# Second scan of a two-layer kernel: the output rows are turned by VectorE in 32x32 blocks instead of by TensorE

## What is computed

```python
x = x + _L0_conv_ref(_gn(x), ...)      # per head: a 128x128 softmax matrix mixes the 128 positions; plus a bias
x = x + _L1_conv_ref(_gn(x), W)        # a scan over h:
# rows = moveaxis(x, 1, 0); row0 = rows[0]
# def step(carry, row):
#     new = row + relu(conv1d_same(carry, W))     # W is (9, 64, 64), along the 128 positions
#     return new, new
```

## Time and profile before

| | us |
|---|---|
| median of 3 runs | 833.74 |
| lowest, highest | 831.69, 834.27 |
| the profiled execution, its own time | 832.51 |
| its span | 830.5 |
| TensorE busy | 740.7 (89%) |
| VectorE busy | 593.0 (71%) |
| ScalarE busy | 479.2 (58%) |
| GpSimd busy | 433.3 (52%) |
| TensorE's granted clock, mean | 0.978 of full speed |

### The profile page before, as it was taken

How to read it: one execution, slowest core, us unless ns; L and a number is a source line. 1 busy time by engine, 2 the same in 40 slices (tenths; PEclk the granted TensorE clock), 3 DMA queues, 4 the chain that set the end, 5 groups by cost and what they waited for, 6 DMA issues and landing times.

```text
span 830.5 us, 17386 instructions
## 1 busy us (share of the span) xinstructions
PE 740.7 (89%) x5546; PEld 705.0 (85%) x5546; DVE 593.0 (71%) x1265; ACT 479.2 (58%) x918; POOL 433.3 (52%) x416
## 2 busy tenths in 40 slices
PE   1577667758999999999999999998999999999997
PEld 1456555648999899999999998988999999999997
DVE  6699999983767878786878787655555555555553
ACT  2156555564666676666666666656555555555552
POOL 1666777762656566656656565643333333333332
PEclk9999999997999999999999999999999999999999
DMA  9845444231334443444434321212222222222222
GB/s 184 157 103 122 108 102 108 45 77 37 85 83 102 91 102 89 91 91 102 101 89 101 87 66 42 52 39 52 65 65 64 63 63 63 63 63 67 66 65 68
DMA packets 203149, 68.11 MB, mean 82 GB/s; under 512 B 137556, under 2 KB 203092, under 8 KB 203092
## 3 DMA queue, kind: packets, MB, share of 16 engines
q1 hardware_dynamic: 203092, 67.43, 37.2%
HBM read 33.85 MB, written 33.55 MB: 81 GB/s over the span
## 4 chain that ended last, share of the span: by engine, by line
PE 73%; DVE 15%; issue 4%; POOL 4%; ACT 2%; DVEq 0%; ACTq 0%; POOLq 0%
PE ps_conv L976 37%; PE ps_conv L980 18%; PE ps_mix L892 7%; PE ps_out L968 7%; DVE st L668 4%; PE ps_in L905 4%; DVE st L550 3%; POOL xs L352 3%; DVE dev L613 2%; PE ps_small L882 1%; DVE x_sb L661 1%; ACT x_paired L438 1%; ACT rows L460 1%; DVE st L562 1%; DVE dev L618 1%
## 5 line engine op out<-in xcount | busy, mean ns | idle before, releaser
L379 POOL TENSOR_TENSOR total<-x_paired,carry 128x256 f32<-128x256 f32 x256 | 188.7, 737 | 305.1 <-DVE carry L758 301.7
L766 DVE TENSOR_TENSOR carry_l<-carry,carry_h 128x256 fp32r<-128x256 f32 x252 | 174.6, 693 | 90.9 <-ACT carry_h L480 90.9
L480 ACT ACTIVATE carry_h<-carry 128x256 fp32r<-128x256 f32 x252 | 105.7, 419 | 228.3 <-DVE carry L758 228.1
L976 PE MATMUL ps_conv<-carry_h,wh 128*128 128x256 f32 x1280 | 219.5, 303 | 5.3 <-ACT carry_h L480 5.3
L438 ACT ACTIVATE x_paired<-ps_in,shift 64x512 f32<-64x512 f32 (+1 forms) x256 | 174.8, 683 | 75.9 <-PE ps_in L905 72.6
L352 POOL TENSOR_TENSOR xs<-x_sb,rstd 128x512 f32<-128x512 f32 x104 | 195.1, 1898 | 38.6 <-DVE rstd L643 38.6
L976 PE MATMUL ps_conv<-carry_h,wl 128*128 128x256 f32 x1280 | 198.3, 285 | 0.0
L980 PE MATMUL ps_conv<-carry_l,wh 128*128 128x256 f32 x1280 | 197.0, 285 | 0.0
L976 PEld LDWEIGHTS ps_conv<-carry_h,wh 128*128 128x128 f32 x1280 | 176.9, 192 | 7.1 <-ACT carry_h L480 5.9
L758 DVE SCALAR_TENSOR_TENSOR carry<-ps_conv,rows 128x256 f32<-128x256 f32 x256 | 107.7, 421 | 105.0 <-PE ps_conv L980 98.9
L976 PEld LDWEIGHTS ps_conv<-carry_h,wl 128*128 128x128 f32 x1280 | 174.5, 191 | 0.0
(11 more groups left out here) (92 smaller groups left out, 401.4 us busy)
## 6 DMA issues: line engine op xcount, KB each, us to landing
out_dram<-staged SPq DMA_DIRECT2D x256, 128.0 KB, 2.4
x_sb<-in_x_dram SPq DMA_DIRECT2D x52, 512.0 KB, 4.1
rows<-in_x_dram SPq DMA_DIRECT2D x12, 512.0 KB, 4.0
x_paired<-in_L_conv_W_dram SPq DMA_DIRECT2D x2, 80.0 KB, 2.7
x_paired<-in_L_conv_W_dram SPq DMA_DIRECT2D x2, 64.0 KB, 2.5
x_paired<-v_attention_centers_dram SPq DMA_DIRECT2D x1, 0.0 KB
x_paired<-v_attention_spreads_dram SPq DMA_DIRECT2D x1, 0.0 KB
bias_col<-v_token_proj_n_bias_dram SPq DMA_DIRECT2D x1, 0.5 KB, 5.3
```

Of the source, the lines that this page charges most:

```text
L379: nc.gpsimd.tensor_tensor(total[s][:, :].rearrange("p (w j) -> p w j", w=WS), x1_rows(wave, it, i, 1, s * WS, WS)[:, 0, :, :], carry[s][:, ...
L766: nc.vector.tensor_tensor(carry_l[s][:, :, EDGE:EDGE + J], carry[s][:, :].rearrange("p (w j) -> p w j", w=WS), carry_h[s][:, :, EDGE:EDGE ...
L976: nc.tensor.matmul(ps_conv[:, s * BANK:s * BANK + SW], w[:, d, :], carry_h[s][:, :, d:d + J], start=(w is wh and d == 0), stop=False)
```

## The change

In the second scan (wave 1) the four TensorE transposes and ScalarE's copy go. VectorE transposes `total[s]` in 32x32 blocks straight into `staged` (`flip_out`), between the carry of a half and its low part. After it a partition of `staged` holds a position, and a run of 32 elements holds 32 channels. Eight DMAs store a row, each from 32 partitions, 8 batches, 128 contiguous bytes at a time (256 runs of 128 bytes). SyncE issues five of them, ScalarE three, behind its second norm of the step. GpSimd's next sum waits for the flip of its half. A flip waits for the stores of the row two before (`flip_stored`). VectorE's first iteration of the second scan is written out. The first scan stays as it is, and so does the turning of its last row.

```diff
+    out_blocks = out.rearrange("b h (jh jl q) c -> b h jh jl q c", jl=BL, q=2)   # BL = 32
+        def flipped_block(wave, h, buf, block):
+            q, half, jh = block // 4, block // 2 % 2, block % 2
+            at = q * C + half * BL
+            dst = out_blocks[wave * W:(wave + 1) * W, bass.ds(h, 1), jh, :, q, half * BL:(half + 1) * BL]
+            src = staged[at:at + BL, buf, :].rearrange("p (m jh c) -> p m jh c", jh=2, c=BL)
+            return dst.rearrange("m h j c -> (h j) m c"), src[:, :, jh, :]
 # SyncE
+            def store_flipped(wave, h, buf):
+                rows_flipped = held(sp, h + 1)
+                alone(sp, w_zeroed)
+                for s in range(NS):
+                    sp.wait_ge(out_flipped[s], rows_flipped)
+                for block in range(SP_BLOCKS):                 # SP_BLOCKS = 5
+                    dst, src = flipped_block(wave, h, buf, block)
+                    sp.dma_start(dst, src).then_inc(flip_stored[buf], 16)
 # GpSimd, add_carry
+                if wave == 1 and not (is_zero(it) and i == 0):
+                    pool.wait_ge(out_flipped[s], it * STEPS + i)
 # ScalarE
+            def store_flipped(wave, h, buf):
+                rows_flipped = held(act, h + 1)
+                alone(act, setup_done)
+                for s in range(NS):
+                    act.wait_ge(out_flipped[s], rows_flipped)
+                for block in range(SP_BLOCKS, BLOCKS):         # BLOCKS = 8
+                    dst, src = flipped_block(wave, h, buf, block)
+                    act.dma_start(dst, src).then_inc(flip_stored[buf], 16)
-                        if s == 0 and not begins:
+                        if s == 0 and wave == 0 and not begins:
                             stage_out(t, (i + 1) % 2)
+                    if wave == 1 and not begins:               # after both halves
+                        store_flipped(1, it * STEPS + i - 1, (i + 1) % 2)
 # VectorE
+            def flip_out(wave, it, i, s):
+                buf = (i + 1) % 2
+                h = it * STEPS + i - 1
+                if isinstance(h, int) and h < 2:
+                    dve.wait_ge(stored[buf], H // 2 * 32)
+                else:
+                    dve.wait_ge(flip_stored[buf], 128 * (it * (STEPS // 2) + (i - 1) // 2))
+                nc.vector.transpose(staged[:, buf, s * SW:(s + 1) * SW],
+                                    total[s][:, :]).then_inc(out_flipped[s], 1)
+                        if wave == 1 and not (is_zero(it) and i == 0):   # between carry and low part
+                            flip_out(wave, it, i, s)
 # TensorE
-                            if s == 0:
+                            if s == 0 and wave == 0:
                                 turn_out(t)
-            turn_out(2 * H)
```

More of the change, by code:

```diff
@@ L53, in mix_and_scan_kernel @@
     x_nat = x.rearrange("b h n c -> n b h c")
+    BL = 32
+    SP_BLOCKS = 5
+    BLOCKS = 8
+    out_blocks = out.rearrange("b h (jh jl q) c -> b h jh jl q c", jl=BL, q=2)
     out_pairs = out.rearrange("b h (j q) c -> b h j (q c)", q=2)
@@ L199, in mix_and_scan_kernel @@
         stored = [sem(f"stored{n}") for n in range(2)]
+        out_flipped = [sem(f"out_flipped{s}") for s in range(NS)]
+        flip_stored = [sem(f"flip_stored{n}") for n in range(2)]
         def x1_unit(wave, b, c, u):
@@ L290, in store_row @@
                                  src[e * J:(e + 1) * J, :, :]).then_inc(stored[buf], 16)
+            def store_flipped(wave, h, buf):
[6 more added lines that the diff above has]
+                    sp.dma_start(dst, src).then_inc(flip_stored[buf], 16)
             def iteration(wave, it, b, e, more):
                 for i in range(STEPS):
-                    if not (is_zero(it) and i == 0):
+                    if wave == 1 and not (is_zero(it) and i == 0):
+                        store_flipped(wave, it * STEPS + i - 1, (i + 1) % 2)
+                    if wave == 0 and not (is_zero(it) and i == 0):
                         store_row(wave, it * STEPS + i - 1, (it + wave * ITERS) * STEPS + i, (i + 1) % 2)
@@ L313, in _ @@
                 iteration(1, it, None, None, 0)
-            store_row(1, H - 1, 2 * H, 1)
+            store_flipped(1, H - 1, 1)
             for n in range(2):
-                sp.wait_ge(stored[n], 2 * H // 2 * 32)
+                sp.wait_ge(stored[n], H // 2 * 32)
+                sp.wait_ge(flip_stored[n], H // 2 * 128)
         @block.gpsimd
@@ L376, in add_carry @@
                 pool.wait_ge(carry_ready[s], t + 1)
-                if not is_zero(t):
+                if wave == 0 and not is_zero(t):
                     pool.wait_ge(out_turned, t)
+                if wave == 1 and is_zero(it) and i == 0:
+                    pool.wait_ge(out_turned, t)
+                if wave == 1 and not (is_zero(it) and i == 0):
+                    pool.wait_ge(out_flipped[s], it * STEPS + i)
                 nc.gpsimd.tensor_tensor(total[s][:, :].rearrange("p (w j) -> p w j", w=WS),
@@ L527, in _ @@
             iteration(1, ITERS - 1, None, None, False, False)
-            stage_out(2 * H, 1)
+            store_flipped(1, H - 1, 1)
         @block.vector
@@ L862, in _ @@
             finish(B - 1, 1)
-            with dve.Fori(0, ITERS - 1) as it:
+            iteration(1, 0, None, None, False, False)
+            with dve.Fori(1, ITERS - 1) as it:
                 iteration(1, it, None, None, False, False)
             iteration(1, ITERS - 1, None, None, False, False)
+            for s in range(NS):
+                dve.wait_ge(total_ready[s], 2 * H)
+                flip_out(1, ITERS, 0, s)
         @block.tensor
```

## The result

The changed kernel takes 807.73 us (median of 4 runs, 805.2 to 808.28) against 833.5 us for the kernel before, measured beside it: a ratio of 0.9688, 95% interval 0.9661 to 0.9714. The forecast was 852 us with a range of 814 to 905. The kernel became faster by 26 us, where 18 us slower was expected. Rival A, which stood at 0.14 and 812 us, is the case that came.

What follows compares the result with a forecast made beforehand. TensorE bound the second scan at 4.09 us a step; after the change, the loop through ScalarE's issues would. Hardware loop +14.9, first iteration -0.9, last 0, end +4.3: +18.3 on 832.5 makes 850.8, so 852 us; range 814 to 905.

Steps and rivals of the forecast that it cites:

- Rival A: Second scan, ScalarE: an issue takes only 0.37 us, so the loop is 3.71 and the total 812 us; chance 0.14.
- Part 2: VectorE in the second scan: two flips a step at 0.43 us fit the 0.49 hole, costing the recurrence nothing.
- Part 3: ScalarE's three issues at 0.60 us close a one-step loop, D + 1.92: 4.40 in the hardware loop, 3.98 written out.
- D: Time from flip 1's end until ScalarE is free again: 2.48 us in the hardware loop, 2.06 written out.
- Part 4: SyncE's five issues: about 4.1 us a row, hidden beside 4.40; the last lands 5.8 us behind flip 1, covered.
- Part 5: Second scan's store transfers: 2048 runs of 128 bytes a row, 16 ns each of one DMA engine, hidden.
- Rival F: Store transfers: 128-byte runs cost as much as 512-byte ones, 4.6 to 4.8 us a row; 871 or more; chance 0.09.
- Part 6: GpSimd's later sum stays hidden; the end after the last carry grows from 6.05 to 10.3 us, 4.3 more.
- B: Hardware loop issues at the written-out pitch: steps of 4.0 to 4.1 us, 832 to 838 in all; chance 0.06.
- C: ScalarE's and SyncE's queues hinder each other in part: one wait of 0.3 us in each D, 871 us; chance 0.21.
- D2: ScalarE's and SyncE's queues take full turns: pitch 1.20 us on both, step 5.82, 948 us in all; chance 0.07.
- E: ScalarE's issues start only when its norm has finished: steps 0.64 us longer, 892 us in all; chance 0.10.

## Why the prediction was wrong

**What bounds the kernel now: right.** TensorE's 4.09 us a step set the second scan. Nothing else was gained than its transposes: 4.09 to 3.64.

**Part 1: right.** 28 us were forecast for TensorE alone. The stretch from first to last carry became 28.3 us shorter.

**Part 2, the flip: right.** It was taken at 0.43 us and took 0.433, with a place in the 0.49 us hole. The estimate worked out from the Trainium skill (VectorE: DVE Perf Modes, The three transpose paths), 0.44, agrees.

**Part 3, the issues on ScalarE: the step that failed.** The loop from the issues over high 0, low 0, carry 1 and flip 1 exists: runs with D = 2.25, 2.62 and 2.76 us gave steps of D + 1.56. But the prediction had it set the pace, at 4.40 us a step, and TensorE set it, at 3.64. Two terms of the loop were mis-sized.
The first is the issue. It was taken at 0.60 with a pitch of 0.79, from the row "of the same direction and nearest shape"; ScalarE's measured 0.35, with a pitch of 0.52. That row is of a 64-partition DMA, and 64 happens to be a slow number. The argument against rival A, "both shapes of fewer than 128 partitions took 0.60", rested on two rows that had 64 partitions both. What they had in common was taken for "fewer than 128", although a third row that the prediction itself quotes, one partition at 0.225, already spoke against that. D was 1.75 and not 2.48. Putting the 0.60 back cost 31 us (839.0 against 807.7).
The second is low 0. It was taken at its 0.76 of the trace of before. There, as in half 0 of the changed kernel, GpSimd's sum has just started. Once D is long, the sum is over before low 0 begins, and low 0 takes 0.42. That makes the way back 1.56, not 1.92. Most of the remaining 13 us between 839 and 852 lies here: with the 0.60 put back D was 0.14 longer than forecast and the way back 0.36 shorter, the step 4.21 on average instead of 4.40, and 48 such steps are 9 us.
With both terms right the loop is 1.75 + 1.56 = 3.31 us, below 3.64, and the sum comes out at TensorE's pace. The point where rival A was to decide, D under 2.17, is 3.64 - 1.56 = 2.08 for "free", and 4.09 - 1.56 = 2.53 for "faster at all". The four runs fit this: with D at 1.75 nothing was lost, at 2.25 the kernel was still faster than before, at 2.62 and 2.76 slower.
Rival A named the right issue time (0.37, D 1.79), but its 812 us are near 808 partly by luck: it closed the same loop with the 1.92 and let it bind at 3.71, where TensorE's 3.64 did.

**Part 4, SyncE: hidden, as said, with more room.** Five issues at a pitch of 0.50, with what stands between the rows, make a row cost 2.69 us, not 4.1. A 32-partition store lands 1.5 us after issue (median), not 2.4. With eight on SyncE this cover goes, and the kernel is 40 us slower than the changed one.

**Part 5, the transfers: right, a little too dear.** 0.45 x 3.64 us x 16 / 2048 is 12.8 ns for a 128-byte run; 16 was taken. Rival F is out.

**Part 6, the ends.** The last carry starts 7.6 us before the end of the span, 6.05 before: 1.5 more, where 4.3 was said, again from issues at half their assumed length.

**The other rivals.** B, the loop at the written-out pitch: for the new stores it is so, 0.50 us in both forms on SyncE, but with issues over 64 partitions put back ScalarE's three took 2.23 us, a pitch of 0.80 in the loop, near the forecast's 0.79. C and D2, the two queues hindering each other: SyncE's issue takes 0.316 us alone and beside ScalarE's; ScalarE's three take 1.39 for a sum of 0.38 + 2 x 0.345 and two gaps, so nobody takes full turns and no wait of 0.3 us stands in D. A small part of C is left. The first of ScalarE's three, which starts together with SyncE's, is the one of 0.38, and beside issues of 0.63 us on ScalarE a fifth of SyncE's took about 0.1 us longer. The Trainium skill (Perfetto Trace Analysis, DMA Instruction — HWDGE) has the descriptor generator locked for exclusive use during an issue; whether that is what these rows show, and how much of an issue it covers, was not measured: ScalarE never issued alone. E, issues that wait for the norm: the first issue starts at 702.33, while the norm behind high 1 still runs: out.

## What to carry to other kernels

Before a DMA issue is priced from a row of the trace, ask what sets that row: here the count of partitions did, and whether the issue stood in a hardware loop; and two rows that agree can share the one property that makes them dear. When a slow engine's queue holds a DMA issue, write the loop out through every in-order queue behind it (issue, high part, low part, carry, flip, issue) and compare its length with the bound; what is left over says how many more issues fit, here not one. A duration taken over from the trace is only as good as its neighbours: if the change moves what ran beside it, it changes.

## What the runs showed of the hardware that was not expected

A store over 64 partitions held SyncE's queue for 0.608 us with each of the run counts and lengths tried; in the hardware loop over 32 or 48 partitions 0.32, over 16 partitions 0.45. Written out and directly behind another issue, these took 0.43 to 0.45 (32 and 48) and 0.59 (16). A load over 128 partitions took 0.37. One store over 64 partitions cut into two over 32 holds the queue longer in the loop: from start to start the two take 1.02 us (704.50 to 705.52 in the run with several shapes), the one 0.81 (705.52 to 706.33). ScalarE's queue needed 0.348 for the shape for which SyncE's needed 0.316, always beside SyncE's, and 0.626 over 64 partitions. ScalarE's sequencer issued DMAs while its engine still executed the instruction ahead (issue at 702.33, norm until 702.68).

VectorE's subtraction of two SBUF tensors (128x256, float32) took 0.43 us alone and 0.75 when it started just behind a sum of the same size on GpSimd; the sum took 0.73 alone and 0.92 when it started second.
